# Feature turns in a Chebyshev and hyperbolic graph kernel: block-diagonal weights on full array rows, one bank in place of two, and a third work bank

## What is computed

```
h = relu(layernorm(x))
T1 = adj @ h;  T2 = 2 (adj @ T1) - h;  T3 = 2 (adj @ T2) - T1
x = x + h @ W0 + T1 @ W1 + T2 @ W2 + T3 @ W3 + bias0
h = relu(layernorm(x));  p = expmap(h)        # tanh of the row norm
s = adj @ p;  x = x + logmap(s) @ K + bias1    # atanh of the row norm
```

## Time and profile before

| what | us |
|---|---|
| three executions | 1758.67, 1759.46, 1760.33 |
| median | 1759.46 |
| the profiled execution, its own time | 1758.64 |
| span of its trace | 1756.70 |
| TensorE busy / VectorE busy / ScalarE busy / GpSimd busy | 1708.7 / 1285.4 / 266.6 / 164.3 |
| HBM traffic | 665 MB, mean 379 GB/s |

### The profile page before, as it was taken

How to read it: one execution, slowest core, us unless ns; L and a number is a source line. 1 busy time by engine, 2 the same in 40 slices (tenths; PEclk the granted TensorE clock), 3 DMA queues, 4 the chain that set the end, 5 groups by cost and what they waited for, 6 DMA issues and landing times.

```text
span 1756.7 us, 66856 instructions
## 1 busy us (share of the span) xinstructions
PE 1708.7 (97%) x30828; PEld 1018.2 (58%) x30828; DVE 1285.4 (73%) x2081; ACT 266.6 (15%) x507; POOL 164.3 (9%) x228
## 2 busy tenths in 40 slices
PE   7999999999999999999999999999999999999997
PEld 5655555555655555555555555566655555656554
DVE  7157777776878687789889886487778776776745
ACT  1013222111111011011100001222110111010014
POOL 0000000000000010211011000111001000000003
PEclk9999999999999999999999999999999999999999
DMA  9999999999999987889999987799999999999996
GB/s 368 420 420 418 419 418 415 414 414 411 403 409 406 397 304 287 334 317 332 340 338 334 339 326 277 273 386 398 411 419 410 406 420 415 418 419 412 419 419 263
DMA packets 95013, 665.13 MB, mean 379 GB/s; under 512 B 11408, under 2 KB 13712, under 8 KB 14608
## 3 DMA queue, kind: packets, MB, share of 16 engines
q1 hardware_dynamic: 93744, 660.64, 94.1%
q10 hardware_dynamic: 992, 0.23, 0.1%
HBM read 658.74 MB, written 2.10 MB: 376 GB/s over the span
## 4 chain that ended last, share of the span: by engine, by line
PE 79%; DMA 12%; DVE 6%; issue 1%; ACT 1%; SPq 1%; POOL 0%; DVEq 0%; ACTq 0%
PE own_bank L788 22%; PE row_bank L788 18%; DMA ring<-adj_blocks 12%; PE work_bank L690 12%; PE row_bank L690 9%; PE work_bank L788 7%; PE turned L690 5%; PE turned L703 2%; DVE ring L1069 1%; PE row_bank L826 1%; PE work_bank L804 1%; PE own_bank L690 1%; DVE ring L1073 1%; PE own_bank L804 1%; PE row_bank L804 0%
## 5 line engine op out<-in xcount | busy, mean ns | idle before, releaser
L1069 DVE TENSOR_TENSOR ring<-ring 128x1024 f32<-128x1024 f32 x323 | 401.8, 1244 | 130.0 <-DMA ring<-adj_blocks 64.1
L788 PE MATMUL own_bank<-ring 128*32 128x256 f32 x5024 | 432.8, 379 | 0.2
L788 PE MATMUL own_bank<-ring,nodes 128*32 128x256 f32 x3768 | 384.2, 379 | 1.3 <-DVE ring L1069 1.1
L788 PE MATMUL row_bank<-ring 128*32 128x256 f32 x3488 | 300.2, 379 | 0.0
L788 PEld LDWEIGHTS own_bank<-ring 128*32 128x32 f32 x5024 | 230.9, 110 | 108.5 <-DVE ring L1073 1.7
L690 PE MATMUL row_bank<-ring,nodes 128*32 128x256 f32 (+1 forms) x3856 | 263.9, 382 | 17.4 <-DMA ring<-adj_blocks 16.1
L788 PE MATMUL row_bank<-ring,nodes 128*32 128x256 f32 x2616 | 266.3, 379 | 3.6 <-POOL ring L649 1.9
L690 PE MATMUL work_bank<-ring,nodes 128*32 128x256 f32 x4288 | 252.4, 380 | 4.8 <-issue 3.1
L1075 DVE TENSOR_TENSOR ring<-ring 128x512 f32<-128x512 f32 x323 | 230.2, 713 | 11.0
L788 PEld LDWEIGHTS own_bank<-ring,nodes 128*32 128x32 f32 x3768 | 189.4, 110 | 83.6 <-DVE ring L1069 4.5
L1073 DVE TENSOR_TENSOR ring<-ring 128x512 f32<-128x512 f32 x323 | 229.1, 709 | 11.1
(11 more groups left out here) (159 smaller groups left out, 1154.0 us busy)
## 6 DMA issues: line engine op xcount, KB each, us to landing
ring<-adj_blocks SPq DMA_DIRECT2D x626, 1024.0 KB, 10.5
out<-resid SPq DMA_DIRECT2D x16, 128.0 KB, 2.9
resid<-x SPq DMA_DIRECT2D x7, 256.0 KB, 12.0
resid<-x SPq DMA_DIRECT2D x2, 128.0 KB, 3.4
w_raw<-cheb_weight ACTq DMA_DIRECT2D x2, 64.0 KB, 9.1
bias<-cheb_bias ACTq DMA_DIRECT2D x1, 32.0 KB, 3.1
bias<-hyp_bias ACTq DMA_DIRECT2D x1, 32.0 KB, 5.1
w_raw<-hyp_kernel ACTq DMA_DIRECT2D x2, 16.0 KB, 9.8
```

Of the source, the lines that this page charges most:

```text
L788: done = nc.tensor.matmul(bank[lane:lane + H, columns], left(a, h, level), right[b][:, h, :], start=first and k < 2, stop=k == 6, tile_pos ...
L1069: nc.vector.tensor_tensor(first_two(n, block), block[:, :, N2].rearrange("p (k h) n -> p k h n", k=2), block[:, 0:2, :].rearrange("p h (k ...
```

## The change

1. The turn weights become block-diagonal: `w_h`, `w_last` and `turn` get one more axis of two. Half 0 holds the weight on partitions 0 to 63 and zeros on 64 to 127, half 1 the other way round. One matmul with all 128 rows and 2 x width moving columns then gives both halves of the nodes. GpSimd zeroes the three tensors ahead of `ident`'s second step, and VectorE fills them with twelve instructions on 64 partitions in place of six on 128.
2. `to_nodes` uses the tile form of the visits (128*64 at first, 128*32 later) and writes one bank; its output is two runs of columns, one for each half.
3. The turns of levels 1 to 3 use `turned[:, 0]` alone. `turned[:, 1]` is a work bank for every `AGAIN` visit, and the planner's condition and the wait of a turn for a work bank's reader (`turn_before`) go.
4. The turns of level 4 go round five single banks instead of three pairs. `H_TERM` writes `work_banks[0]` alone.

The order of the steps, the loads and the data are the same.

```diff
-            n = in_order.index(i) + 1
-            between = kind == "AGAIN" and i < first_out and not any(n - 2 < t < n + 2 for t in turn_at)
-            free = [k for k in range(2) if pair_ended and held_until[k] < i] + [2] * between
+            free = [k for k in range(2) if pair_ended and held_until[k] < i] + [2] * (kind == "AGAIN")
...
-            turn_before[i] = bank_user[2][2] if bank_user[2] and bank_user[2][0] == "SPILL" else 0
-            bank_user[2] = ("TURN", i, turns)
...
-        w_h = sb("w_h", [P, F])
-        w_last = sb("w_last", [P, F])
-        turn = sb("turn", [P, 3, 2 * F])
+        w_h = sb("w_h", [P, 2, F])
+        w_last = sb("w_last", [P, 2, F])
+        turn = sb("turn", [P, 3, 2, 2 * F])
...
-        out_pairs = [turned, own_pair, row_pair]
+        turn_bank = turned[:, 0, :]
+        out_banks = [turn_bank, *own_banks, *row_banks]
...
             nc.gpsimd.memset(ident[:, :], 0.0).then_inc(s_zeroed, 1)
+            for weights in (w_h, w_last):
+                nc.gpsimd.memset(weights[:, :, :], 0.0).then_inc(s_blank, 1)
+            nc.gpsimd.memset(turn[:, :, :, :], 0.0).then_inc(s_blank, 1)
...
-            def to_nodes(pair, source, weight):
+            def to_nodes(bank, source, weight):
                 width = weight.shape[-1]
+                to = bank[:, 0:C * width].rearrange("p (h k n) -> p h k n", h=2, k=2)
                 for k in range(2):
-                    for lane in range(0, P, TURN_SIZE):
-                        for half, rows in enumerate((ODD, EVEN)):
-                            at, to = k * P + lane, (1 - half) * (BLOCK - 2 * width) + k * width
-                            done = nc.tensor.matmul(pair[lane:lane + TURN_SIZE, half, to:to + width],
-                                                    source[rows, at:at + TURN_SIZE], weight[rows, :], start=k == 0, stop=k == 1,
-                                                    tile_position=(half * F, lane), skip_group_check=True)
+                    for lane in range(0, P, size):
+                        done = nc.tensor.matmul(to[lane:lane + size, :, k, :], source[:, k * P + lane:k * P + lane + size],
+                                                weight, start=k == 0, stop=k == 1, tile_position=(0, lane),
+                                                skip_group_check=True)
...
-                    if turn_before[i]:
-                        pe.wait_ge(s_spilled, turn_before[i])
...
+                dve.wait_ge(s_blank, 3)
+                for half, rows in enumerate((ODD, EVEN)):
+                    nc.vector.tensor_tensor(w_h[rows, half, :], w_raw[rows, 0, :], w_raw[rows, 2, :], ALU.subtract)
...
```

More of the change, by code:

```diff
@@ L302, in chebyshev_hyperbolic_kernel @@
     visit_no, turn_no, spill_no, row_bank, own_bank = {}, {}, {}, {}, {}
-    work_bank, bank_user, bank_before, turn_before = {}, [None] * 3, {}, {}
+    work_bank, bank_user, bank_before = {}, [None] * 3, {}
     held_until = [-1] * 3
@@ L342, in chebyshev_hyperbolic_kernel @@
     pair_ended, last_own, turned_by = False, None, None
-    turn_at = [sum(t[0] in VISITS for t in steps[:i]) for i, s in enumerate(steps) if s[0] == "TURN"]
-    first_out = next(i for i, s in enumerate(steps) if s[0] == "TURN" and s[2] == 4)
     for i, s in enumerate(steps):
@@ L565, in chunks, with by_chunks @@
             return slice(r * C, (r + 1) * C)
-        def by_chunks(pair, width=P):
-            both = pair[:, :, :].rearrange("p b n -> p (b n)")
-            return both[:, BLOCK - 2 * width:BLOCK + 2 * width].rearrange("p (c n) -> p c n", c=C)
+        def by_chunks(bank, width=P):
+            return bank[:, 0:C * width].rearrange("p (c n) -> p c n", c=C)
         H = F // 2
@@ L675, in wait_for_work_bank @@
                         pe.wait_ge(s_spilled, n)
-                    elif reader == "TURN":
-                        pe.wait_ge(s_read, n)
                     elif reader == "OWN":
@@ L877, in _ @@
                     source = partial[:, r, N1] if level == 4 else acc[:, acc_buf[r, level] % 2, :]
-                    weight = w_last if level == 3 else turn[:, min(level - 1, 2), :]
-                    if turn_before[i]:
-                        pe.wait_ge(s_spilled, turn_before[i])
+                    weight = w_last[:, :, :] if level == 3 else turn[:, min(level - 1, 2), :, :]
                     if level < 4:
-                        out_pair = turned
+                        out_bank = turn_bank
                         if t > 1:
@@ L895, in _ @@
                         pe.wait_ge(s_acc, acc_no[r, level])
-                    pe.wait_ge(s_terms, 1)
-                    done = to_nodes(out_pair, source, weight)
+                    pe.wait_ge(s_terms, 2)
+                    done = to_nodes(out_bank, source, weight)
                     done.then_inc(s_turned, 1)
@@ L966, in _ @@
                     r, n = s[1], out_turn[s[1]]
-                    pair = by_chunks(out_pairs[n % len(out_pairs)])
+                    pair = by_chunks(out_banks[n % len(out_banks)])
                     act.wait_ge(s_turned, turn_no[r, 4])
@@ L1009, in weight_terms @@
                 dve.wait_ge(s_w, 6 * 16)
[L1010 to L1016 removed]
+                dve.wait_ge(s_blank, 3)
+                for half, rows in enumerate((ODD, EVEN)):
+                    nc.vector.tensor_tensor(w_h[rows, half, :], w_raw[rows, 0, :], w_raw[rows, 2, :], ALU.subtract)
+                    nc.vector.tensor_tensor(turn[rows, 0, half, F:], w_raw[rows, 1, :], w_raw[rows, 3, :], ALU.subtract)
+                    nc.vector.tensor_scalar(turn[rows, 1, half, F:], w_raw[rows, 2, :], 2.0, None, ALU.mult)
+                    nc.vector.tensor_copy(turn[rows, 2, half, F:], w_raw[rows, 4, :])
+                    nc.vector.tensor_scalar(w_last[rows, half, :], w_raw[rows, 3, :], 2.0, None, ALU.mult)
+                    nc.vector.tensor_copy(turn[rows, :, half, 0:F],
+                                          ident[rows, rows].unsqueeze(1).to_broadcast([F, 3, F])).then_inc(s_terms, 1)
             added = {}
             deviations = len(H_GROUPS)
[L1020 removed]
+            wide = by_chunks(turn_bank)
             def to_halves(to, by_levels, level, by_halves, op=ALU.add):
@@ L1227, in _ @@
                         dve.wait_ge(s_spilled, spill_no[h_term])
-                    terms = by_chunks(turned, F) if level == 3 else wide[:, :, F:]
+                    terms = by_chunks(turn_bank, F) if level == 3 else wide[:, :, F:]
                     nc.vector.tensor_tensor(own_resid, own_resid, terms, ALU.add).then_inc(s_read, 1)
```

22 lines of the change are left out of this document (7 added, 15 removed).

## The result

| | before | changed |
|---|---|---|
| median, 19 executions each | 1759.36 us | 1762.43 us |
| lowest and highest | 1757.83, 1761.38 | 1760.53, 1764.74 |
| ratio, 95% interval | | 1.0017 (1.0011 to 1.0024) |
| span of the profiled execution | 1756.7 us | 1760.9 us |

The change costs 3.1 us, 0.17%. The forecast was +2.5 us and 1762.0 us, counted as no change as it is under 0.2%. The measured time lies inside the forecast's own range of 1760.5 to 1763.3, and the difference is small but not zero by its interval. The number is close, but two of its terms are off and largely cancel, as the experiments show; the agreement of the sum says less than it seems to.

The account below looks back on a forecast made before the run. Loads set the pace to some 412 us, TensorE from 424 to 1080, loads tied to TensorE by dips from 1240, TensorE again from 1703. 3.1 - 0.8 - 1.9 + 2.1 = +2.5 us gave 1762.0 us; overall range 1757.5 to 1765.5.

Parts of the forecast that it names:

- The wide turn: Turns of levels 1, 2 and 4: 0.74 to 0.865 us each; 25 between 424 and 1080 us cost +3.1 us.
- The narrow turn: Turns of level 3: 0.53 to 0.47 us, gaining 0.06 (0.02 to 0.10) each; 14 on the path give -0.8 us.
- The third bank: Around 1320 and 1370 us: two 1.54 us work-bank waits go, each giving back 0.6 in mixing waits; -1.9 us.
- the last dip: Load-rate dip at 1580 to 1590 us, 386 GB/s: TensorE's gains or losses until then are kept, savings up to 1700 lost.
- rival A: Third bank brings nothing if the load queue is the limit from 1320 us; 1763.9 to 1764.7 us, chance 0.27.
- The tail: From 1700 us: fourteen level 4 turns cost 1.75 us and the longer last turn 0.40; +2.1 us.
- The sum: Whole kernel: 3.1 - 0.8 - 1.9 + 2.1 = +2.5 us, giving 1762.0 us against the median.
- The start: Extra GpSimd zeroing and VectorE instructions push TensorE by up to 1.4 us, hidden by loads until 412 us; nothing added.
- C: New turns' output in two runs of columns with a gap slows their matmuls; 41 us more, 1803 us, chance 0.03.
- E: Weight loads of new turns don't run under their matmuls; 24 us more, 1786 us, chance 0.01.
- B: Turns hide first rounds under the preceding visit, or mixing waits don't appear; 1760.2 us (chance 0.08) or 1755.3 (0.05).
- D: Planner still hands out held banks, or new turns keep 0.3 us seams, 12 us; 1774 us, chance 0.02.

Follow-up runs that it names:

- e12: The kernel before with each turn of level 2 issued twice in a row; 1766.20 us against 1758.98, ratio 1.0041.
- e11: The changed kernel with all turns in tiles of 128 rows x 64 columns, visits staying 128 x 32; 1773.35 us against 1758.98 for the kernel before, ratio 1.0082.
- e3: The kernel before, old turns, planner counting a bank held for an OWN visit as used until its JOIN; 1758.78 us against 1759.20, ratio 0.9998.
- e1: The changed kernel run again with no edit; 1762.61 us against 1759.20 for the kernel before, ratio 1.0017.
- e5: The changed kernel with late blocks (first needed from some 1200 us) loaded to seven eighths only; 1758.23 us against 1759.14 for the kernel before, ratio 0.9995.
- e8: The kernel before with level 3 turns and H_TERM in the new form, wide turns old, held banks counted as used until their JOIN; 1758.46 us against 1759.14, ratio 0.9996.
- e10: The kernel before with 26 warm-up matmuls in place of 10; 1759.34 us, ratio 1.0001.
- e2: The changed kernel with the old planner's choice of banks, so new turns only; 1761.83 us, ratio 1.0016 to the kernel before.
- e4: The kernel before with turns in tiles of 64 rows x 32 columns in place of 64 x 64; 1770.23 us, ratio 1.0063.

## Why the prediction was right, and where it was not

**The wide turn.** 0.74 us to 0.865 us; measured 0.86. Confirmed, and the split of the old turn by e12, the price of a change of form by e11. Between 475 and 1085 us the changed kernel falls back from 0.74 to 3.44 us, 2.7 us for 24 wide turns, 0.11 each.

**The narrow turn.** Forecast -0.06 us, measured 0.53 to 0.43, and -0.085 from turn to turn: 14 of them gave 1.2 us and not 0.8. The middle between the bounds was the wrong pick. The lower bound came from rounds of the same tile form, the upper from rounds of 128*64 tiles; the row with the same form was the nearer one.

**The third bank.** The two waits were named rightly, and so was what comes next, the 0.59 us at L1062. Both waits had 1.54 us and gave a net 0.95 each by 1378 us. The step that failed is the next one: "what it has won or lost up to the last dip is carried on". It rests on the sentence that "a dip means that a slot came free late", and that was not read from any row. In the dip of the earlier trace rows, from 1580 to 1590 us, three to five blocks are on their way at each moment, and the five loads issued around it took 10.7 us to land (median), where one block at 420 GB/s takes 2.5. That dip is no gap in the queue that an earlier TensorE could fill. Only at 1347 us does the number fall to two, with 344 GB/s for 2 us; above that one block more is worth 3 to 6 GB/s, 1%. What makes the deeper dips is not known; e3 and e1 have theirs too. The experiments e1, e3 and e5 to e8 show what follows: TensorE's 1.5 to 1.8 us of lead are gone by the turn of 1562 us in e3, at the block that lands at 1552 us. I had this as rival A with its mechanism and place, and gave it half the chance of the other branch on the ground that TensorE "never waits for a block" there. That is no argument: an engine that just doesn't wait is at the wall, not far from it. What should have been read is how long a block has landed when its visit starts (0.3 us at 1551.55), and whether the queue of loads ever runs empty.

**The tail.** Forecast +2.1, of which 14 wide turns and the longer last turn came as stated (2.37 us late at the first turn of level 4 in e1, 3.3 us at the last, then 0.4 more in the span). But between the turns at 1722.82 and 1726.03 us of the old trace the distance shrinks by 0.62 us: the old kernel's stall of 0.75 us has gone. I had seen the stall and found no wait for it, and left it out of the sum. Where it stood is shown by e10. That the change took it away because the new form wants 37 instructions a us where the old one wanted 39 is likely but not shown: four traces with the new tail have no stall, e2's has two.

**The sum.** Read off e1: 2.4 us at the end of the loads in place of 0.4, and +1.3 behind it in place of +2.1. So +2.5 was forecast, and 3.7 in that trace and 3.1 to 3.4 in the medians were measured. The errors of +2.0 and -0.8 share the outcome with the spread, and that they pull against each other is luck. With the wall in place of the third bank the sum would go: 2.9 us late at 1234 us, where the wall begins; the narrow turns behind it and the third bank bring nothing, and the landings of e1 stay 2.5 to 3.0 us late; 1.3 behind the loads; 3.8 to 4.2 us. Measured are 3.7 us between the two traces, of which the one before is of an execution 0.7 us below its median, and +2.6 (1.2 to 4.4) in e2's median. So no run tells the small terms apart to better than some 0.5 us.

**The start.** VectorE's six more instructions took 0.9 us (15.40 to 17.1 against 15.24 to 16.1), TensorE runs up to 1.5 us late at 50 us in e1 (2.7 in the first trace, where the granted clock was at half from 26.2 to 29.6 us), and at 103 us it is level in both: hidden by the loads, as stated.

**Rivals.** C (the output in two runs) and E (weight loads in the open) fall with the 0.86 us. B falls too: no turn hides rounds under its neighbours, and both bank waits gave back their mixing wait. For E stood the Trainium skill's rule ("TensorE: Matmul & The Clock Gate", "What overlaps and what doesn't") that weight loads overlap only across row groups; visits and turns, all in one row group, contradict it alike (0.216 us a round, with four loads of 0.11 us to each). D falls with the form in the rows.

## What to carry to other kernels

When an engine's waits for a transfer are near zero and the transfers run at their full rate, look whether it stands at a wall: read how long each transfer has landed when it is used, and whether there is ever a moment with none under way. If the first is near zero and the second never comes (here never fewer than two), count savings of the engine in that stretch as nothing until something is taken off the transfers. A long time from issue to landing alone doesn't tell: it was 5.7 us (median) between 430 and 1080 us too, where TensorE set the pace. A small operation in another tile form costs its seams (0.29 us here) besides its columns, so twice the columns in the neighbours' form may cost about the same; price both from the distance between the neighbours' starts. And list stalls that no semaphore explains, with their count of instructions from the start: an edit that puts instructions ahead of them moves them.

## What the runs showed of the hardware that I had not expected

- TensorE's instructions come in blocks of 256, and a stall that no semaphore explains stands at one and the same place of a block (fourteen of fourteen in the tails). In e4's tail, at 128 instructions for each visit and turn, stalls of 1.4 us stand every 6.5 us, exactly 256 instructions apart. At 39 a us they are few and short (one of 0.75 us before, four of 0.2 to 1.1 us in e10), at 37 a us there are none in four tails and two of some 0.5 us in e2's.
- A wait can cost more than its length: behind 2.35 us of waiting the granted clock was at 1.2 GHz for 3.4 us and the visit took 3.54 us in place of 1.93. Behind 1.53 us in e1 it stayed at 2.4 GHz.
- A change of column width alone, 128*32 to 128*64 and back, costs 0.29 us, as much as a change of rows.
- A matmul of 256 columns whose output lies in two runs of 512 bytes with a gap takes 0.379 us, the same as one with a single run.
